# Expert layers: the gather of chunk 2 is issued ahead of the base's accumulating transfers

## The reference

```python
# layer 0: capacity of 512 tokens an expert
scores = softmax(xf @ w_router); expert_weights, top_experts = top_k(scores, 2)
h = gelu(einsum('ech,ehf->ecf', xb, w1)); y = einsum('ecf,efh->ech', h, w2)
out = zeros((T, hs)).at[src].add(flat_w[order][:, None] * yv) + bias
# layer 1: all tokens
h = gelu(einsum('td,edh->eth', xf, W1) + b1); expert_out = einsum('eth,ehd->etd', h, W2) + b2
out = einsum('etd,te->td', expert_out, softmax(masked_logits))
x = x + ffn(layernorm(x), ...)
```

## Time and profile before

| | before |
|---|---|
| median of 3 runs | 2554.02 us |
| lowest and highest | 2550.81 and 2555.0 us |
| the profiled execution's own time | 2552.48 us |
| its span, first to last instruction | 2550.7 us |
| TensorE busy over the span | 2288.7 us (90%) |
| mean granted clock of TensorE | 0.969 of full speed |
| expert loop of layer 0 begins | about 1480 us |
| expert loop of layer 1 begins | about 2257 us |

### The profile page before, as it was taken

The page is one execution under the profiler, slowest core; times in us unless marked ns, Lnnn a source line. Parts: engine busy times, 40 slices in busy tenths (PEclk is TensorE's granted clock), DMA queues, the critical chain, the costliest instruction groups (busy, mean ns, idle before and its releaser), DMA issues. The chain is left out here.

```text
span 2550.7 us, 48415 instructions
## 1 busy us (share of the span) xinstructions
PE 2288.7 (90%) x16979; PEld 1394.3 (55%) x16980; DVE 1919.7 (75%) x3499; ACT 1900.7 (75%) x2979; POOL 1809.4 (71%) x1580
## 2 busy tenths in 40 slices
PE   5999999999999999999998589978988888689998
PEld 3454545444544545455544368845555555467777
DVE  7888778887778887777786556558899899676443
ACT  4787887878877878778787546638888889767555
POOL 2687877787777878787778567617787789646554
PEclk9999999999999999999999789989999999779999
DMA  5000000000000000000000365441112010375221
GB/s 151 1 1 1 27 1 1 1 1 1 27 1 1 1 1 1 1 1 1 1 1 1 107 154 144 115 102 45 46 34 50 22 43 11 105 187 140 44 42 24
DMA packets 90655, 104.49 MB, mean 41 GB/s; under 512 B 20626, under 2 KB 79971, under 8 KB 90419
## 3 DMA queue, kind: packets, MB, share of 16 engines
q1 hardware_dynamic: 68180, 78.21, 10.2%
q0 software_dynamic: 21696, 23.16, 5.7%
q10 hardware_dynamic: 544, 0.00, 0.0%
HBM read 66.65 MB, written 23.52 MB: 35 GB/s over the span
## 5 line engine op out<-in xcount | busy, mean ns | idle before, releaser
L432 POOL TENSOR_TENSOR a_acc<-a_acc,a_pf 128x512 f32<-128x512 f32 (+1 forms) x480 | 680.1, 1417 | 280.2 <-ACT a_pf L601 258.5
L906 DVE TENSOR_TENSOR a_pl<-a_pf,a_ph 128x512 f16<-128x512 f32 x448 | 470.3, 1059 | 25.1 <-ACT a_ph L607 25.1
L2221 POOL TENSOR_TENSOR c_pl<-c_pf,c_ph 128x512 f16<-128x512 f32 x320 | 377.2, 1210 | 117.1 <-ACT c_ph L2318 116.7
L601 ACT ACTIVATE a_pf<-a_psS 128x1024 f32<-128x1024 f32 (+1 forms) x288 | 281.1, 976 | 110.0 <-PE a_psS L624 102.5
L882 DVE TENSOR_REDUCE a_mx<-a_psA 128x1 f32<-128x512 f32 x504 | 330.4, 680 | 26.8 <-PE a_psA L681 25.5
L607 ACT ACTIVATE a_ph<-a_psS 128x1024 f16<-128x1024 f32 (+1 forms) x288 | 281.1, 976 | 0.0
L553 ACT ACTIVATE a_psS<-a_mb 128x1024 f32<-128x1024 f32 x255 | 248.6, 975 | 5.0
L1317 DVE TENSOR_TENSOR f_xn<-f_xn 128x256 f16<-128x256 f32 x312 | 130.0, 423 | 152.0 <-ACT f_xn L1286 106.8
L2554 DVE TENSOR_REDUCE c_wf<-c_psA 128x1 f32<-128x512 f32 x384 | 239.4, 677 | 6.2 <-PE c_psA L2390 5.3
L2311 ACT ACTIVATE c_pf<-c_psS 128x1024 f32<-128x1024 f32 x192 | 201.2, 1048 | 49.6 <-PE c_psS L2419 45.1
L776 PE MATMUL a_psO<-a_pl,a_vh 128*128 128x512 f16 (+1 forms) x544 | 206.9, 380 | 8.1 <-POOL a_pl L450 7.9
(11 more groups left out here) (366 smaller groups left out, 6311.4 us busy)
## 6 DMA issues: line engine op xcount, KB each, us to landing
f_stage<-in_L_ffn_w SPq DMA_DIRECT2D x16, 1024.0 KB
f_stage<-in_L_ffn_W SPq DMA_DIRECT2D x16, 1024.0 KB
c_kst<-c_khs SPq DMA_DIRECT2D x64, 100.1 KB, 2.2
a_cx<-in_ctx SPq DMA_DIRECT2D x4, 1536.0 KB
c_cx<-in_ctx SPq DMA_DIRECT2D x12, 512.0 KB, 4.0
f_xrow<-f_xn SPq DMA_DIRECT2D x8, 512.0 KB, 4.6
c_kst<-c_kls SPq DMA_DIRECT2D x32, 100.1 KB, 2.2
X<-in_x SPq DMA_DIRECT2D x4, 512.0 KB, 10.3
```

The source lines that it names most:

```text
L432: g.tensor_tensor(acc[0:k, p, :], acc[0:k, p, :], pf[0:k, q % RF, i, :], ALU.add).then_inc(s_acc, 1)
L601: act.activation(pf[0:r, q % RF, 0:k, :], psS[q % 2][0:r, 0:k, :], ACT.Exp, scale=SCALE).then_inc(s_pF, 1)
L906: v.tensor_tensor(pl[0:r, q % RP, i, :], pf[0:r, q % RF, i, :], ph[0:r, q % RP, i, :], ALU.subtract).then_inc(s_pL, 1)
L2221: g.tensor_tensor(pl[0:r, q % RP, i, :], pf[0:r, q % RF, i, :], ph[0:r, q % RP, i, :], ALU.subtract).then_inc(s_pG, 1)
```

## The change

GpSimd issues the gather and the weights of chunk 2 before the base's four transfers instead of behind them. What each transfer moves stays as it is. For every later chunk the order stays: gather of chunk n + 2, then scatter of chunk n. The two waits are also split, so that the one on the gate stands behind the row gather and in front of the weights, which is the case for all chunks.

```diff
             gather_weights(0)
             gather(1)
             gather_weights(1)
+            def ahead(n):
+                g.wait_ge(main.xP, n + 3)
+                gather(n + 2)
+                g.wait_ge(s_gate, n + 1)
+                gather_weights(n + 2)
+
+            ahead(0)
             if layer:
                 g.wait_ge(s_wbF, NT // 2)
                 add_base(lambda q: wb[:, 4 * q:4 * q + 4, :])
...
             for n in range(NC):
-                if n + 2 < NC:
-                    g.wait_ge(main.xP, n + 3)
-                    g.wait_ge(s_gate, n + 1)
-                    gather(n + 2)
-                    gather_weights(n + 2)
+                if n and n + 2 < NC:
+                    ahead(n)
                 if n == 0:
                     g.wait_ge(s_bst, 16 * NQ)
                     g.wait_ge(s_sidx, 1)
```

## The result

The changed kernel took 2557.08 us (median of 22 runs, 2548.07 to 2564.98), the kernel before 2552.33 us in the same sets of runs (22, 2545.36 to 2557.86). The ratio of the runs is 1.0021, with a 95% interval of [1.0014, 1.0028], or +5.4 us. The profiled execution of the changed kernel took 2557.15 us (span 2555.1), 4.65 us more than the one before (2552.5).

What follows compares the result with a forecast made beforehand. TensorE was taken to bound layer 0; layer 1 lost 4.36 us around the reordered transfers, DMA engines full. Layer terms 5.1 + 2.2 = +7.3 us on 2552.5 gave 2559.8; the median's 1.5 us made 2561.3 us, range 2552.5 to 2567.

Steps and rivals of the forecast that it cites:

- The waits on the turn and the gate cost nothing: GpSimd, chunk 2's issues: both moved waits are met when reached; cost nothing, or 0.3 us if GpSimd is quicker.
- The base holds the first scatter, and chunk 3's rows are behind it: GpSimd's queue: the scatter waits for the late base with chunk 3's gather behind it, so TensorE's wait moves by one chunk.
- By how much the scatter is late in layer 0: First scatter, layer 0: base issued 5.0 us later and sharing with a 2.6 us load; 6.4 us late.
- From the last row issue to the turn: Chunk 3's rows, both layers: usable 3.5 us after their last issue, bounds 2.2 and 4.8.
- The clock: TensorE behind layer 0's gap at chunk 3: the granted clock falls, costing 1.7 us (bounds 0 and 1.7).
- Layer 0: Chunk 3's turn there: TensorE waits 3.4 us for rows and loses 1.7 us of clock, +5.1 us.
- Layer 1's gain: Around chunk 2's turn: waits of 3.42, 1.98 and 1.25 us and the clock loss go, at most 4.36 us.
- Layer 1's loss: Chunk 3's turn there: scatter 4.2 us later, rows late; +1.4 us and 0.8 us of clock, +2.2 us.
- A: Rival: same wait at chunk 3 but small, rows land in 2.2 us, no clock lost; 2554.5 to 2559, chance 0.24.
- B: Rival: the base's delay is hidden, layer 1 wins 4.36 us, layer 0 loses nothing; 2549 to 2552, chance 0.10.
- C: Rival: the wait at its upper bound in both layers, 13.1 us; 2566 to 2570, chance 0.05.
- D: Rival: both effects real and cancelling, +2 in layer 0, -2 in layer 1; 2553 to 2555, chance 0.11.

Runs made afterwards that it cites:

- gathers_pass_scatters: Changed kernel with every gather from chunk 3 on issued before the scatter it stood behind; ratio 1.0010, +2.5 us against the kernel before.
- chunk3_ahead_too: Changed kernel with chunk 3's gather also issued before the first scatter, behind the base; ratio 1.0010, +2.6 us against the kernel before.
- layer0_base_early: Changed kernel with layer 0's base added before all gathers, layer 1 as changed; ratio 1.0022, +5.6 us against the kernel before.
- quarter_base: Changed kernel with only the first of the base's four transfers in each layer, output incomplete; 2530.04 us in one run.
- the third set: Later runs in which the kernel before (2535.2 or 2535.5 us in the later sets) and the changed kernel were timed and profiled again; ratio 1.0039, +9.9 us.
- the first pair: The first two profiled executions, unmodified kernels: the kernel before at 2552.5 us and the changed kernel at 2557.15 us.
- load_behind_base: Changed kernel with SyncE holding layer 0's loads of experts 2 and up until the base has landed; 2544.47 us in one run.
- layer0_only: New order in layer 0 alone, layer 1 in the old order; ratio 1.0033, +8.4 us against the kernel before.
- rows_only_ahead: Changed kernel with only chunk 2's two row gathers ahead of the base, its weight gathers behind it; 2537.41 us in one run.
- the first set: First group of follow-up runs, each compared with its own runs of the kernel before, which took 2553.4 us there.
- the second set: Second group of follow-up runs, with no trace of the kernel before; that kernel took 2535.2 or 2535.5 us in the later groups.
- old_order_chunk3_ahead: Kernel before (base first, then chunk 2's gather) with chunk 3's gather also before the first scatter; ratio 1.0011, +2.8 us.

## Why the prediction was right, and what it mis-sized

The mechanism is the one forecast. That the total came out near the forecast is partly luck. By the turns both layers lost more than predicted: layer 0 7.05 us at chunk 5 (predicted 5.1) and layer 1 3.40 us at chunk 4 (predicted 2.2), together 10.4 us against 7.3. Between these two traces only 4.65 us remain, mainly because layer 1 of the kernel before had more long chunks behind chunk 4. The pair without such chunks shows 9.9 us.

**The waits on the turn and the gate cost nothing.** Right: the base's issue in layer 1 begins at 2270.26 with no wait in front of it, 8.52 us after the turn of chunk 0.

**The base holds the first scatter, and chunk 3's rows are behind it.** Right in both layers and in each trace of the changed order. The undoings point the same way. Take the gathers from behind the scatter, and the wait goes (gathers_pass_scatters). Take one, and it moves to the next (chunk3_ahead_too). Get the base out of the way, and it goes (layer 0 of layer0_base_early, both layers of quarter_base).

**By how much the scatter is late in layer 0.** Predicted 6.4 us (bounds 2.6 and 7.6), measured 7.7, just past the upper bound; in the third set it was 27.27 - 18.75 = 8.5. Taken apart: the issue later by 5.0 us is right (5.4 in the first pair, 3.25 to 8.61 us after chunk 0's turn; 3.55 to 8.51, or 5.0, in the third set). The 2.6 us of sharing with a load is right (2.5 to 2.9, load_behind_base). The trace shows how they share. From 1499 to 1502, with the base and the load of 1493.73 both in flight, the changed kernel moves (queue, packets, MB, share of the engines):

```profile
q1 hardware_dynamic: 193, 0.78, 69.0%
q0 software_dynamic: 198, 0.20, 40.5%
```

The packets are equal in number, but this load's are of 4 KB and the base's of 1 KB, so the load goes at 260 GB/s and the base at some 67, a third of its 197. By an estimate from these rates the load takes 4.0 us, in which the base falls 2.7 us behind.

What was short is the base without a load beside it. By the prediction it takes 1502.2 + 1.2 - 1488.7 = 14.7 us from its first issue to the scatter; load_behind_base took 15.84, and the kernel before 15.20 in the third set, where the scatter waited for the base itself. In the trace read for the prediction the scatter waited for chunk 0's output, so the base's end was not to be seen there, and it was put some 0.5 to 1.1 us early.

**From the last row issue to the turn.** Predicted 3.5 us (2.2 to 4.8). Measured 2.9 in layer 0, 5.1 in layer 1, 4.9 in load_behind_base with two loads beside it. So the wait came out at 4.29 us (predicted 3.4, bounds 0 and 5.9): the later scatter and the shorter landing went against each other. The Trainium skill (DMA: Bandwidth & Descriptors, section on the anatomy of one DMA) gave an estimate of 2.3 us for these bytes. The trace is 0.6 us above it at the landing of 2.9 us and more than twice it beside loads, so a landing was better taken from a row with the same neighbours than from the formula.

**The clock.** The step was right and its size too small: predicted 1.7 us, measured 14.19 - 11.42 = 2.8 in layer 0, and 14.20 - 11.30 = 2.9 in the third set. Two stretches of 1 us of the changed kernel, at the wait and in the loss:

```profile
1514.00:1515.00 1.00, 0.21 (x1) 0.22 (x2) 0.00 (x0) 0.00 (x0) 0.70 (x2) 0.50 0.02 2
1520.00:1521.00 1.00, 1.00 (x8) 0.78 (x7) 0.51 (x2) 0.44 (x2) 0.80 (x1) 0.68 0.45 131
```

The granted clock falls to its lower level, 1.2 GHz, near the end of a gap of 4.29 us and is back at 2.4 GHz only during the slice at 1520. The 1.7 us had been read behind a gap of 1.98 us, and after the longer gap the low stretch was longer. A gap of 4.41 us gave 13.90 - 11.36 = 2.5 (layer0_only). So the loss does not follow the length of the gap exactly. Shorter gaps behind a wait for rows in layer 0: 3.79 us gave 14.12 - 11.30 = 2.8 (load_behind_base), 3.47 gave 13.02 - 11.42 = 1.6 (chunk3_ahead_too), 1.67 gave 11.41 - 11.30 = 0.1 (rows_only_ahead).

**Layer 0** was put at +5.1 us and came out at +7.05 (first pair) and +8.1 (third set). The terms mis-sized are the wait, +0.9 (a base end put too early, less a landing taken too long), and the clock, +1.1, in the first pair.

**Layer 1's gain.** 4.36 us of earlier turns was put as the most that could be won, and it was to be eaten by the wait at chunk 3. The settled distance of 12.48 us behind that figure was one of the long chunks: later ones of the same trace take 11.35 to 12.93 us, and nearly all of the third set 11.30, so that up to 5.5 us stood there. In the first pair chunk 2's turn came no earlier, 25.81 us against 25.06. The load of the first gap came in time, but TensorE had a gap of 1.64 us behind ScalarE at 2274.94 that the trace puts down to no load, with 1.2 GHz granted for some 3 us behind it, and ScalarE then waited 3.21 us for the load issued at 2275.05. The prediction had said that ScalarE's wait for a load is gone; it had moved to the next load. A gap of the same kind (1.63 us) stands in the one other trace of the new order whose chunk 2 is as late (25.56 us, chunk3_ahead_too). In the third set 2.09 us of the gain were there and had gone by the next turn. Over the runs with the new order and the whole base in layer 1 the turn of chunk 2 lies anywhere from 19.65 to 25.81 us, while that of chunk 3 lies at 40.4 to 41.1 in six of eight (37.94 in chunk3_ahead_too, 43.34 in layer0_base_early), whether its rows wait for 0 or for 2.8 us. The kernel before has 36.88 and 37.84.

**Layer 1's loss.** Predicted +1.4 for the turn and 0.8 for the clock, +2.2. Measured +3.0 at the turn of chunk 3 and +0.4 more for the clock at chunk 4 in the first pair, +3.5 and +3.6 in the third set, +2.3 there at the layer's end. The scatter was 3.5 us late (predicted 4.2), and 29.31 - 24.61 = 4.7 in the third set. Two terms were short. The landing of 5.1 us is above the upper bound of 4.8, and from the scatter to the end of the last row issue it took 7.4 us and not 6.7. And the contention of the later base with the loads of the first experts is a second way to lose the same microseconds; the prediction counted those loads only as a delay of the base and not the base as a delay of them. The runs show it most plainly where the rows wait for nothing: 5.96 us of ScalarE's time (gathers_pass_scatters).

**The rivals.** A (a small wait) needed a scatter less than 4 us late in layer 0; it was 7.7. B (the base's delay is hidden) fails on the scatter times: they are 7.7 and 3.5 us late. C's size was approached in the third set, with 9.9 us of its 13.1, by a longer clock loss than C allowed and without both waits at their bound. D fails as a mechanism, since layer 1 gives nothing back at chunk 4. That the first measurement, +5.4, is nearer to it than the +9.9 of the third set goes, as far as the traces show, with the uneven chunks.

**What stays open:** what lengthens single chunks of layer 1 from 11.6 to 12.9 us in the first pair and the first set (the record numbers the chip of the first and the second set alike, 4, so a difference between chips does not explain it); the gap of 1.64 us behind ScalarE at 2274.94; and chunk 2 of old_order_chunk3_ahead.

## What to carry to other kernels

A queue that is served in order passes a delay on to whatever stands behind the instruction that waits. Before issues are swapped, look for the next instruction in that queue that waits for the one moved back, and for the work behind it; here bringing one gather forward by 5 us made the next one late. Where the DMA engines were full, the order chose only which transfer was late: count the bytes between two due times first, and try the small transfer between the pieces of the large one (here that cost nothing, and its gain is not shown) before moving it ahead of the whole. And price a stall of an engine whose clock can fall by rows behind a gap of about its length and with about the same work in front: 4.3 us of waiting cost 7.1.

## What the runs showed of the hardware that was not expected

- Two transfers from different queues share the engines packet for packet and not byte for byte. Beside the base's 1 KB packets a load in 4 KB packets went at 260 GB/s (193 packets against 198 in 3 us), and a load in 1 KB packets at 120 GB/s (822 against 825 in 7 us). The base alone moves at 197 GB/s and a load alone at 397. So 1 MB in small packets took 13.4 us from issue to use in layer0_base_early, with 3.7 us of it before its packets began to move (at 2276.2). The Trainium skill (DMA: Bandwidth & Descriptors, section on queues, rings and completion order) says that each engine takes turns between its queues by packets. The trace agrees, as far as equal counts of the profile's packets show it.
- The granted clock stayed low for longer behind 4.3 us of idleness than behind 2 us (2.8 against 1.7 us lost). The length of the gap did not decide it alone. Behind 1.67 us in layer 0 of rows_only_ahead, with TensorE busy for 0.79 and 0.99 of the two microseconds before, the clock held at 1.00. Behind 1.64 us in layer 1 of the changed kernel, with TensorE busy for 0.61 and 0.72 of the two microseconds before, it was 0.50 for the three slices behind it.
- The same kernel took 2553.4 us in one set of runs and 2535.2 in another. In the traces the chunks of layer 1 differ most: 11.6 to 12.9 us against a steady 11.30. The change cost 5.4 us in the first measurement and 9.9 in the third set, so a difference of 0.2% of a kernel is itself not a constant.
